# float32r products of two parts and two heads on the array's rows, in a three-stage transformer kernel

## What is computed

```
tokens = einsum('npi,di->npd', patches, W_map) + b_map      # then class token, positions
x = (tokens - mean) / sqrt(var + eps) * ln_w + ln_b         # mean and var over the whole image
q, k, v = xh @ Wq + bq, xh @ Wk + bk, xh @ Wv + bv          # per head: 12 heads of 16
msa = softmax(q @ k.T / sqrt(16)) @ v
h = tokens + msa                                            # input of the second attention
q, k, v = h @ W_qkv                                         # 192 x 576
out = softmax(causal(q @ k.T * 16**-0.5)) @ v @ W_out + b_out
# then layer norm, routing to 64 slots, an expert per slot (192 -> 768 -> 192), combination, layer norm
```

## Time and profile before

| | us |
|---|---|
| median of 3 runs | 5457.48 |
| lowest and highest | 5455.46, 5478.61 |
| span of the profiled execution | 5457.1 |
| embedding, first to last use of L349 | 33.4 to 1029.2 |
| first attention, first to last use of L710 | 1068.0 to 2733.5 |
| causal attention, first to last use of L710 | 2814.3 to 4165.0 |
| routing, first to last use of L1089 | 4207.0 to 4868.7 |
| experts, first to last use of L1306 | 4913.7 to 5211.4 |
| last pass, first to last use of L1433 | 5236.0 to 5452.9 |

### The profile page before, as it was taken

How to read it: one execution, slowest core, us unless ns; L and a number is a source line. 1 busy time by engine, 2 the same in 40 slices (tenths; PEclk the granted TensorE clock), 3 DMA queues, 4 the chain that set the end, 5 groups by cost and what they waited for, 6 DMA issues and landing times. The chain is left out here.

```text
span 5457.1 us, 157255 instructions
## 1 busy us (share of the span) xinstructions
PE 5137.1 (94%) x48514; PEld 4451.1 (82%) x48514; DVE 3369.8 (62%) x9562; ACT 2687.3 (49%) x6788; POOL 1826.7 (33%) x2821
## 2 busy tenths in 40 slices
PE   8999999799999999999979999999997888889987
PEld 7999999677777777777758888888886777779965
DVE  4555555566666666666636666666665666650069
ACT  3444444255555555555525555555554666653400
POOL 2343333233333333333312222222222444431145
PEclk9999999899999999999969999999998555559965
DMA  5766667666666666666636666666663222229977
GB/s 143 174 174 173 174 173 174 143 150 149 153 151 150 153 149 152 153 148 153 146 85 133 131 130 132 131 131 131 131 131 81 66 67 66 67 64 271 276 211 215
DMA packets 701721, 789.03 MB, mean 145 GB/s; under 512 B 362639, under 2 KB 514989, under 8 KB 701646
## 3 DMA queue, kind: packets, MB, share of 16 engines
q1 hardware_dynamic: 701646, 788.10, 61.3%
HBM read 518.50 MB, written 265.72 MB: 144 GB/s over the span
## 5 line engine op out<-in xcount | busy, mean ns | idle before, releaser
L710 DVE TENSOR_REDUCE a_mx<-a_sq 99x2 f32<-99x394 f32 x1536 | 798.5, 562 | 165.2 <-PE a_sq L764 159.8
L710 DVE TENSOR_REDUCE c_mx<-c_sq 99x2 f32<-99x198 f32 (+1 forms) x1536 | 656.9, 462 | 267.0 <-PE c_sq L764 253.0
L662 ACT ACTIVATE a_ex<-a_sk 99x792 f32<-99x792 f32 (+1 forms) x768 | 639.3, 833 | 202.9 <-PE a_sk L794 171.0
L662 ACT ACTIVATE c_ex<-c_sk 99x792 f32<-99x792 f32 (+1 forms) x768 | 511.9, 667 | 336.6 <-PE c_sk L794 230.7
L399 PE MATMUL e_tokp<-e_wmap,e_ptT 128*99 128x192 f32 x3072 | 530.3, 330 | 1.0 <-ACT e_ptT L304 1.0
L399 PEld LDWEIGHTS e_tokp<-e_wmap,e_ptT 128*99 128x99 f32 x3072 | 491.8, 167 | 2.3 <-ACT e_ptT L304 1.3
L764 PE MATMUL a_sq<-a_ks,a_qs 96*99 96x198 bf16 x3072 | 429.2, 254 | 39.9 <-DVE a_vx L694 27.4
L761 PE MATMUL c_sq<-c_maskb,c_identb 99*99 99x198 bf16 x1536 | 383.2, 261 | 40.8 <-DVE c_bout L700 27.3
L764 PE MATMUL c_sq<-c_ks,c_qs 96*99 96x99 bf16 (+1 forms) x3072 | 416.2, 232 | 0.0
L794 PE MATMUL a_sk<-a_qs,a_ks 99*99 99x198 bf16 (+1 forms) x3072 | 404.8, 253 | 6.8 <-issue 6.8
L863 PE MATMUL a_work<-a_hT,a_wqkv 96*96 96x198 f32 x2048 | 390.9, 333 | 4.5 <-DVE a_rest L725 2.5
(11 more groups left out here) (178 smaller groups left out, 11867.6 us busy)
## 6 DMA issues: line engine op xcount, KB each, us to landing
e_patches<-in_x SPq DMA_DIRECT2D x128, 588.0 KB
x_w<-in_fc SPq DMA_DIRECT2D x128, 576.0 KB, 5.8
scr_qk<-e_parts SPq DMA_DIRECT2D x128, 445.5 KB
scr_qk<-a_parts SPq DMA_DIRECT2D x128, 445.5 KB
scr_tv<-e_tv SPq DMA_DIRECT2D x128, 297.0 KB
a_tv<-scr_tv SPq DMA_DIRECT2D x128, 297.0 KB
scr_tv<-a_res SPq DMA_DIRECT2D x128, 297.0 KB
c_tv<-scr_tv SPq DMA_DIRECT2D x128, 297.0 KB
```

The source lines that it names most:

```text
L662: nc.scalar.activation(to, of, ACT.Exp).then_inc(exped.sem, 1)
L710: nc.vector.reduce_max(mx[:, b2.parity, qt, h:h + 2], sq[f % 2][:, :, 0:width], AX.X).then_inc(maxed.sem, 1)
```

## The change

*Parts.* q and k are written as two float32r parts (`high`, `low`) instead of three bf16 ones. A head's stack is now 3 x 16 = 48 rows: high, low, high of the queries against high, high, low of the keys, and two rows for the maximum instead of three. Two heads lie in one tile, on partitions 0 to 47 (49 with the maximum) and 64 to 111 (113). The middle part, and POOL's share of the splitting, is gone; ACT makes the high part, DVE the low one.

*Scores.* `query_score` and `key_score` work on one half of the rows (c = 0 or 1). The new function `scores` issues them alternately, a query product of half c and a key product of half 1 - c. Each such product is marked for an array that is split into two halves of 64 rows; masks, transposes and projections use the whole array, `value_products` its four column groups, as before. In the causal pass the half-width products are 100 columns instead of 99, and all masks of a slot's key scores are issued ahead of its products.

*Embedding.* The host lays x out transposed (768 x 198, six rows per partition) and pads it; the 12 transposes and the copies out of PSUM are gone. ACT copies x into a float32r tile xh, POOL subtracts it into xl, and 36 float32r products (xh by high and low weights, xl by high weights) take the place of 12 fp32 ones. xn is turned in three chunks of 64 columns and stacked, high above low, in `stack`; q and k are 6 products, v 12, and the biases are added by ACT and DVE when they take the results out. The pipeline is 5 deep instead of 3.

*First attention.* h is kept as high and low part (hh, and hz for columns 128 to 191, high above low); each 128 columns of q and k take 5 products, v 10.

*Set-up and transfers.* At the start of both attentions DVE fills all of ks with ones (before: its last three rows), and SP's first loads of q and k wait for that. Per image q and k are loaded by 8 transfers instead of 6, 912 KB instead of 891, and stored by 2 of 297 KB instead of one of 445.5 KB; the maximum takes 4 instead of 3. The negative maximum's high part is made by ACT, its low part by DVE, nothing by POOL.

The diff, cut to its core:

```diff
+                b1, b3, b4 = c - 1, c - 3, c - 4
+                if b3.inside(n):
+                    act.wait_ge(mean_s.sem, mean_s.at(b3))
+                    for t in range(2):
+                        nc.scalar.activation(junk[:, t], tv[:, b3.place, 0, t], ACT.Square, bias=st[:, b3.parity, 1:2],
+                                             accum_out=st[:, b3.parity, 2 + t:3 + t]).then_inc(squares.sem, 1)
+                if b4.inside(n):
                     for i in range(2):
+                        act.wait_ge(x_turned.sem, x_turned.at(b4, i + 1))
+                        nc.scalar.copy(stack[0:64, b4.parity, 2 * i:2 + i], xtp[i][:]).then_inc(x_high.sem, 1)
+                if b1.inside(n):
+                    act.wait_ge(loaded.of(b1), loaded.at(b1))
+                    act.wait_ge(embedded.sem, embedded.at(b1 - 2))
+                    nc.scalar.copy(xh[:, b1.parity], xin[:, b1.place]).then_inc(kept.sem, 1)
+                if b3.inside(n):
+                    act.wait_ge(var_p.sem, var_p.at(b3))
+                    nc.scalar.activation(st[:, b3.parity, 4:5], statp[:, 1:2], ACT.Sqrt, bias=eps[:, 0:1]).then_inc(std.sem, 1)
+                if b4.inside(n):
+                    act.wait_ge(stored.of(b4 - 4), stored.at(b4 - 4))
+                    act.wait_ge(qk_done.sem, qk_done.at(b4))
...
+                    dve.wait_ge(mean_p.sem, mean_p.at(b3))
+                    nc.vector.tensor_copy(st[:, w, 1:2], statp[:, 0:1]).then_inc(mean_s.sem, 1)
+                    dve.wait_ge(mean_s.sem, mean_s.at(b3))
...
+                    dve.wait_ge(std.sem, std.at(b3))
+                    nc.vector.reciprocal(st[:, w, 5:6], st[:, w, 4:5]).then_inc(rstd.sem, 1)
...
+                    dve.wait_ge(embedded.sem, embedded.at(b2))
+                    dve.wait_ge(stored.of(b2 - 4), stored.at(b2 - 4))
+                    nc.vector.scalar_tensor_tensor(out=tv[:, b2.place, 0], in0=tokp[b2.parity][:], scalar=1.0, in1=posb[:],
...
+                if b4.inside(n):
+                    for g in range(3):
+                        dve.wait_ge(high.sem, high.at(b4))
+                        nc.vector.scalar_tensor_tensor(out=parts[:, b4.place, 1, g], in0=qk_of(g), scalar=bqk[:, g:g + 1],
+                                                       in1=parts[:, b4.place, 0, g].bitcast(F32), op0=ALU.add,
+                                                       op1=ALU.subtract).then_inc(low.sem, 1)
+                    dve.wait_ge(v_done.sem, v_done.at(b4))
...
+            def embed(b, t):
+                cols = slice(t * TT, (t + 1) * TT)
+                for k in range(KC):
+                    nc.tensor.matmul(tokp[b.parity][:, t], xh[:, b.parity, k, cols], wmaph[:, 0, k], start=(k == 0), stop=False)
+                    nc.tensor.matmul(tokp[b.parity][:, t], xh[:, b.parity, k, cols], wmaph[:, 1, k], start=False, stop=False)
+                    mm = nc.tensor.matmul(tokp[b.parity][:, t], xl[:, b.parity, k, cols], wmaph[:, 0, k], start=False,
+                                          stop=(k == KC - 1))
+                return mm
...
-        qs = m.sb(X + "qs", [AUG, R, HEADS, SP], BF16)
+        qs = m.sb(X + "qs", [128, R, HC, SP], FR)
...
+            def query_score(b, k, c, j):
+
+                qt, g = k // 3, k % 3
+                keys = TT + 1 if causal and qt == 0 else SP
+                rows = slice(64 * c, 64 * c + ROWS)
+                return nc.tensor.matmul(sq[c][:, j, 0:keys], qs[rows, b.place, 3 * j + g, qt * TT:(qt + 1) * TT],
+                                        ks[rows, b.place, 3 * j + g, 0:keys], start=not causal, stop=True,
+                                        skip_group_check=causal)
...
+                first = TT - 1 if causal and kt else 0
+                width = SP - first
+                rows = slice(64 * c, 64 * c + ROWS + 2)
+                return nc.tensor.matmul(sk[k % 2][0:TT - kt, c, j * width:(j + 1) * width],
+                                        ks[rows, b.place, 3 * j + g, kt * TT:kt * TT + TT - kt],
+                                        qs[rows, b.place, 3 * j + g, first:SP], start=not causal, stop=True,
...
+            def scores(bq, bk, k):
+
+                q_in, k_in = bq.inside(n), bk.inside(n)
+                if k_in:
+                    if k < 2:
+                        pe.wait_ge(exped.sem, exped.at(bk - 1, 5 + k))
+                    else:
+                        pe.wait_ge(exped.sem, exped.at(bk, k - 1))
+                    if causal:
+                        key_mask(k)
+                for half in range(2):
+                    if q_in:
+                        if k < 1:
+                            pe.wait_ge(maxed.sem, maxed.at(bq - 1, 11 + half))
+                        else:
+                            pe.wait_ge(maxed.sem, maxed.at(bq, 2 * k + half - 1))
                         if causal:
+                            query_mask(k, half)
+                    for j in range(2):
+                        if q_in:
+                            mm = query_score(bq, k, half, j)
+                            if j:
+                                mm.then_inc(scored_q.sem, 1)
+                        if k_in:
+                            mm = key_score(bk, k, 1 - half, j)
+                            if half and j:
+                                mm.then_inc(scored_k.sem, 1)
...
+                            for g in range(2 * i, 2 + i):
+                                cols = slice(128 * g, 128 * (g + 1))
+                                mm = product(qkp[:, g - 2 * i], [(w1[:, 0, cols], hh[:, 0]), (w1[:, 0, cols], hh[:, 1]),
+                                                                 (w1[:, 1, cols], hh[:, 0]), (w2[:, 0, cols], hz[:]),
+                                                                 (w2[:, 1, cols], hz[:])])
...
-            nc.vector.memset(ks[STACK:AUG], 1.0).then_inc(ready, 1)
+            nc.vector.memset(ks[:].bitcast(F32), 1.0).then_inc(ready, 1)
...
+    xT = np.zeros((x.shape[0], INPUT, SP), np.float32)
+    xT[:, :, 1:SEQ] = np.ascontiguousarray(x).reshape(x.shape[0], PATCHES, INPUT).transpose(0, 2, 1)
```

602 lines of the change are left out of this document (268 added, 334 removed).

## The result

The changed kernel takes 7255.13 us (median; 7229.29 to 7265.35) against 5456.47 us of the kernel before: 1.329 times as long, 95% interval 1.326 to 1.331. The forecast was 5330, range 4900 to 5760.

What follows compares the result with a forecast made beforehand. PE's program per image was taken to bound embedding and both attentions. 5457 less 107 (embedding) and 218 (first attention) plus 172 (causal attention) is 5304; depth (14 us) and set-up (10 us) make 5330, range 4900 to 5760.

Steps and rivals of the forecast that it cites:

- at full clock: All three stages: PE's products, weight loads and row-split changes priced at full clock, such as 0.088 us per 198-column bf16 product.
- forecast of 11.9 for the causal attention: Causal attention: PE's sum of 11.4 us plus 0.5 of waits, against 10.56 before, a loss of 172 us.
- One pass for float32r: PE: a float32r product passes once over its columns, as bf16 does, 0.088 us at any width up to 198.
- 0.112 for 128 stationary columns: PE: a float32r product with 128 stationary columns takes about 0.112 us, set by its weight load.
- pairs side by side: Attention scores: a query and a key product run together on the two row halves, 24 pairs of 0.088 us, 2.1 an image.
- weight loads in turn: Attention scores: row halves share the loading path, 48 loads take 4.2 us instead of 2.1; 5750 us in all; chance 15%.
- slow float32r: All three stages: float32r takes 0.168 us per 198 columns, as one fp32 record; about 6100 us in all; chance 8%.
- The 24 us for more depth and set-up: Two more images of depth in the embedding, 14 us, and longer set-up of both attentions, 10 us.
- A change of the row split: Both attentions: switching the array's row split costs PE 0.11 us at full clock, between 0 and 0.18.
- cheap changes: Both attentions: switching the row split costs nothing that shows; 4945 us in all; chance 19%.
- the ring: Embedding: ACT and DVE steps that follow each other take 6.6 us, 7.0 with handovers, per image; gain 107 us.
- Forecast 11.3 laid out by hand: First attention: PE 9.5 and DVE 8.8 us, with waits between them a period of 11.3 us; gain 218 us.

Runs made afterwards that it cites:

- e3: Changed kernel with both query masks of a slot issued ahead of its eight split products, 12 row-split changes per image for the scores instead of 24: 6993.58 us.
- e10: Changed kernel with split heads filling 64 rows of their half and all four masks of a slot ahead of its eight split products: 6058.77 us.
- e6: Changed kernel with scores unsplit on the whole array and the heads' stacks filled up to 99 rows: 5943.07 us.
- e1: Whole computation left out of the changed kernel, PE alone running stretches of products: plain float32r 0.094 us each, pattern of the causal scores 0.90 us a turn.
- e4: Changed kernel with the low part of x left out, GpSimd subtracting two columns per image instead of 1188: 7258.31 us.
- e16: Changed kernel with q and k's scratch reordered so each store goes to 128 consecutive DRAM rows, stacks loaded by twelve transfers instead of eight: 6947.41 us.
- e13: Whole computation left out of the changed kernel, SP alone issuing stores in several forms: same bytes 96 GB/s as 4 x 32 rows, 355 as 128 rows.
- e17: Changed kernel with both unsplit scores of 99 rows and stores of 128 rows: 5622.60 us, ratio 1.029 to the kernel before.
- e2: Changed kernel with scores unsplit in both attentions, all heads on rows 0 to 66 with zeros on rows 48 to 64: 7423.15 us.
- e5: Whole computation left out of the changed kernel, PE alone running products with various row and column counts: one bf16 with two 64-row pairs 0.575 us a turn.
- e12: Whole computation left out of the changed kernel, SP alone issuing the embedding's transfers: load and stores 172 GB/s, loads alone 412, stores alone 118.
- e9: Changed kernel with split heads filling 64 rows of their half, same number of row-split changes: 7170.73 us.

## Why the prediction was wrong

**The step that failed** stands at the head of the prices: everything on PE was priced "at full clock". The kernel before showed 1.00 in its three stages, and the prediction carried it over to a program whose score products reach over 48 rows instead of 96 and whose array goes in and out of the row split twelve times per image in the causal attention. It had the fact in hand: it used the routing stage, which reads 0.50, to price a change, and did not ask why that stage is at 0.50. What the runs showed in its place: 0.50 through the whole causal attention and 0.78 in the first. The clock alone is 19.37 less 12.65 (e3 and e10), 6.7 us an image or 860 of the 1799 us.

At 2.4 GHz the forecast of 11.9 for the causal attention would still have been too low. e10 took 12.65 with half of the row split's changes; the other twelve at 0.15 to 0.165 make some 14.5 of it (estimate; no run had all 24 changes at full clock). The unsplit products of e6 took 11.39.

**Right as put.** One pass for float32r (0.094 at 198 columns alone, 0.088 to 0.090 in the embedding's 192), 0.112 for 128 stationary columns (e1: 55.7 / 499), pairs side by side (0.093 per pair), so the rivals *weight loads in turn* and *slow float32r* are both out. The 24 us for more depth and set-up met 26.2 by luck in part: 15.9 of these lie between the causal attention and routing, where the forecast had nothing.

**Mis-sized.** A change of the row split: 0.11 forecast, 0.15 to 0.165 measured at full clock, within the stated 0 to 0.18. With 29 of them that is 1.2 to 1.6 us an image in the causal stage: the rival *cheap changes* is out, and the loss there would have been seen at full clock too.

**Embedding.** Forecast 7.0 from the ring. Two terms were wrong. e_xn was taken at 1.06 from the earlier trace rows; beside a subtraction of 1188 columns on GpSimd it takes 2.5 to 2.8 (e4: 0.62 without). With the 2.82 of e16's trace in its place the ring's sum is 8.7, above the 7.99 measured there, so other terms of it are 0.7 too high. And the transfers were passed over with "some 220 GB/s, under the 276 GB/s of the expert stage": the rate of another stage with other shapes. The form in which the parts are stored gave 96 alone. That form was in the diff; the Trainium skill's rule that stands under e13 (DMA: Bandwidth & Descriptors) was not applied to it.

**First attention.** Forecast 11.3 laid out by hand; 15.16 measured. With clock and stores repaired and the pairs undone it is 2.1 less (e17: 13.09 at 1.00). The other 1.8 stay: in e17 PE is busy for 927.92 of 1000 us, that is 12.1 us an image, where the prediction's prices give 9.5, or 10.6 without the pairs (2.1 more) and without nine changes (1.0 less). DVE waits for ACT's a_parts and PE's a_work. Which handover it is was not tried.

**Rivals.** None of them was what happened. The one on the slower side ended at 5750 since it too was priced at full clock.

## What to carry to other kernels

Look at the granted clock of every stage before pricing anything, and ask of a change what it leaves on TensorE: rows, columns, gaps, changes of the split. Products that reach over fewer rows can cost the clock of everything beside them. Rows that are zeros in one operand took no time on PE here and gave the clock back in the causal attention (7423 to 5943 us). A pattern that keeps the clock alone need not keep it inside the kernel. For every store whose form changes, look at the outermost dimension on the DRAM side, and take a transfer's rate only from rows with the same shape.

## What the runs showed that was not expected

- TensorE at 1.2 GHz for 2700 us while busy without a gap (1000.00 of 1000 us): "busy" on the page is no promise of the clock.
- Rows that hold zeros in one operand count for the clock (e2 and e6). 99 rows with only 64 moving columns, alone and without a gap, ran at 0.50 (e5).
- The same bytes from the same tile at 96 or 355 GB/s, by the order of two dimensions in a DRAM scratch (e13). A DMA share of 0.51 with a backlog behind it (e12): the mean over 16 engines hides it when only some of them work.
- Two causes that look like one (rows and changes): in the causal attention, repairing either left the clock at 0.50 (e3, e9), both together brought 1.00 (e10).
